# Second layer of a two-layer recurrent and attention network: the pass for row maxima runs nine slots ahead of the scores instead of eight

## The reference

```
xn = layernorm(x)                       # layer 0
s  = selective scan over the 512 tokens, 16 states per feature, gated, projected
g  = silu(mixture of 8 experts, top 2, gelu, 512 wide)
x  = x + s * g
xn = layernorm(x)                       # layer 1
s  = causal softmax attention, one head of 128
h  = xn + latent attention(rmsnorm(xn)) # 16 heads of 64, causal, keys and values from a latent of 16
g  = silu(h + mixture of 8 experts, top 2, 64 wide, and one shared expert, of rmsnorm(h))
x  = x + s * g
```

```
att = q @ k.T / 8 ; att = where(causal, att, -inf)
p   = exp(att - rowmax(att)) ; y = (p @ v) / rowsum(p)
```

## Time and profile before

| | us |
|---|---|
| median of 3 runs | 1270.45 |
| lowest, highest | 1266.95, 1274.91 |
| the profiled execution, its own time | 1278.83 |
| its span, first to last instruction | 1276.9 |
| PE busy in the span | 1093.6 |
| DVE busy | 961.0 |
| ACT busy | 623.0 |
| first scores of slot 0, in the trace | 407.55 |
| exponentials of slot 191, in the trace | 1232.3 |

### The profile page before, as it was taken

One profiled execution on the slowest core, in us unless ns is written; L12 is line 12 of the kernel. 1 busy time (PEld: TensorE's weight loads), 2 busy tenths in 40 slices (PEclk: granted clock), 3 DMA queues, 4 the chain that ended last, 5 costly groups with the idle time before them and its releaser, 6 DMA issues.

```text
span 1276.9 us, 19206 instructions
## 1 busy us (share of the span) xinstructions
PE 1093.6 (86%) x6753; PEld 691.8 (54%) x6753; DVE 961.0 (75%) x1490; ACT 623.0 (49%) x1111; POOL 306.7 (24%) x371
## 2 busy tenths in 40 slices
PE   7669999999676878889788988998998889899897
PEld 6557887888333434544544554464464346446454
DVE  6757887988367886888788798889889878654424
ACT  2647758565323534346545453654553552353531
POOL 2065554551312300410320231032033021000000
PEclk9769999999887789899988988997898999999998
DMA  7667777775325252345325433543433530130010
GB/s 188 188 198 252 227 228 221 233 225 167 117 53 138 77 125 68 94 116 118 101 69 115 126 103 90 113 126 85 99 105 112 110 84 27 37 65 28 16 45 17
DMA packets 97069, 150.24 MB, mean 118 GB/s; under 512 B 26984, under 2 KB 55984, under 8 KB 96912
## 3 DMA queue, kind: packets, MB, share of 16 engines
q1 hardware_dynamic: 73840, 72.33, 22.6%
q0 software_dynamic: 22976, 76.43, 19.6%
q10 hardware_dynamic: 160, 0.26, 0.1%
HBM read 124.33 MB, written 11.54 MB: 106 GB/s over the span
## 4 chain that ended last, share of the span: by engine, by line
PE 37%; DVE 20%; issue 7%; ACT 5%; DMA 2%; POOL 2%; SPq 0%; another core or an unknown queue 0%; DVEq 0%; ACTq 0%; POOLq 0%
PE bank L1245 8%; DVE neg_max L1767 4%; PE bank L1274 3%; PE bank L1325 3%; DVE sc_state L298 2%; PE bank L1339 2%; PE bank L1334 2%; PE bank L1293 2%; ACT probs L1569 2%; PE bank L1251 2%; PE bank L1329 2%; DMA q_all<-turned_rows 2%; PE bank L1253 2%; DVE sc_y L315 1%; PE bank L1316 1%
## 5 line engine op out<-in xcount | busy, mean ns | idle before, releaser
L1569 ACT ACTIVATE probs<-bank 128x1024 f32<-128x1024 f32 (+1 forms) x192 | 169.3, 882 | 285.6 <-PE bank L1251 204.0
L1767 DVE TENSOR_REDUCE neg_max<-bank 128x2 f32<-128x1024 f32 (+3 forms) x256 | 203.4, 815 | 131.4 <-PE bank L1251 81.3
L1245 PE MATMUL bank<-q_all,kk 49*128 49x512 f32 (+3 forms) x1024 | 203.2, 496 | 48.6 <-ACT probs L1569 30.1
L212 POOL DMA_DIRECT2D sc_bc_wide<-scan_bc x128 | 73.0, 572 | 442.8 <-DVE sc_ub L291 238.8
L1245 PEld LDWEIGHTS bank<-q_all,kk 49*128 49x128 f32 x1024 | 86.6, 194 | 150.3 <-ACT probs L1569 56.7
L1293 PE MATMUL bank<-kr,q_all 48*128 48x512 f32 (+3 forms) x512 | 115.5, 487 | 45.5 <-DVE neg_max L1767 45.2
L779 PE MATMUL bank<-xcol,wst 128*128 128x256 f32 x624 | 149.9, 384 | 0.6 <-ACT xcol L841 0.6
L298 DVE TENSOR_TENSOR_SCAN sc_state<-sc_a,sc_ub 128x1024 f32<-128x1024 f32 x64 | 145.9, 2280 | 0.0
L900 POOL DMA_INDIRECT xrow<-sorted_in,token_of x78 | 103.3, 1325 | 121.2 <-PE bank L766 64.1
L779 PEld LDWEIGHTS bank<-xcol,wst 128*128 128x128 f32 x624 | 114.2, 193 | 13.6 <-issue 0.9
L1274 PE MATMUL bank<-probs,vaug 128*32 128x512 f32 (+3 forms) x1024 | 98.9, 484 | 0.0
(11 more groups left out here) (307 smaller groups left out, 1803.5 us busy)
## 6 DMA issues: line engine op xcount, KB each, us to landing
sc_bc_wide<-scan_bc POOLq DMA_DIRECT2D x128, 512.0 KB
wst<-in_wexp SPq DMA_DIRECT2D x39, 512.0 KB
q_all<-q_kind SPq DMA_DIRECT2D x94, 128.0 KB, 4.3
rec_wide<-head_recips SPq DMA_DIRECT2D x31, 256.0 KB
p_t<-gates_turned SPq DMA_DIRECT2D x14, 512.0 KB
sorted_out<-xrow SPq DMA_DIRECT2D x7, 640.0 KB
rows_all<-in_x SPq DMA_DIRECT2D x8, 256.0 KB, 5.6
sorted_in<-rows_all SPq DMA_DIRECT2D x8, 256.0 KB, 5.6
```

What stands on the lines that cost most here:

```text
L1245: mm(bank[1][:, par, at:at + n], kk[rows, b % 2, kt * P:(kt + 1) * P], q_all[rows, quad // 2 % 3, pair, kt * P:L].bitcast(F32), start=(at ...
L1569: af(probs[:, slot % RING, :, 0:width], bank[1][:, :, 0:width], ACT.Exp, scale=0.125).then_inc(s["p_ready"], 1)
L1767: last = v.tensor_reduce(neg_max[:, quad % 2, pr:4:2, i], bank[0][:, :, at:at + (i + 1) * P], AX, ALU.max, negate=True)
```

## The change

LEAD becomes 9. The whole pass for maxima, its reductions, the transposes (L1304), ScalarE's copies (L1581) and the DMAs (L1140) move one slot earlier against everything else; the first maxima come in slot -9, the last in slot 182. The transpose moves from the slots 4 mod 6 to the slots 3 mod 6. In slot 39 of a batch bank 7 is therefore in use by the transpose; the gates 3 and 4 go to banks 5 and 6 in place of 7 and 5, and the first up product to bank 7 in place of 6.

```diff
-LEAD = 8
+LEAD = 9
...
                     if (b := due(slot, "gates_b")) is not None and b < B - 1:
-                        gate_part(b, 3, 7)
-                        gate_part(b, 4, 5)
+                        gate_part(b, 3, 5)
+                        gate_part(b, 4, 6)
                     if (b := due(slot, "ups_a")) is not None and b < B - 1:
-                        up_part(b, 0, 6)
+                        up_part(b, 0, 7)
...
-                        silus(b, 3, 5, (7, 5))
+                        silus(b, 3, 5, (5, 6))
...
-                        hidden(b, 0, 6)
+                        hidden(b, 0, 7)
```

## The result

The changed kernel takes 1287.77 us (median of 4 runs, 1285.61 to 1291.86), beside 1270.1 for the kernel before in the same session (4 runs, 1266.95 to 1274.91). The ratio is 1.0132, with a 95% interval from 1.0098 to 1.0166: slower, where the forecast had 0.7% and no change that could be told. The forecast, 1279, is missed by 8.8 us; the time lies in the range, next to rival 1 (1286.5). In a second session the changed kernel took 1288.88 (1282.34 to 1295.25), ratio 1.0123 [1.0085, 1.016].

What follows compares the result with a forecast made beforehand. The bound was taken as a path crossing between TensorE and VectorE, neither alone. Terms -5.0 - 2.0 + 13.7 + 3.0 - 1.0 + 0.5 = +9.2 us on 1270.45 gave 1279 us, range 1264 to 1290.

Steps and rivals of the forecast that it cites:

- rival 1: Slots 33 to 153, 9 mod 24: the lower clock follows TensorE's idle 2.3 us each time; +16, 1286.5 us, chance 0.22.
- The bank wait: Slots 9 mod 24: `turn2` waits for bank 7 until ScalarE copies the maxima after the exponentials; loss of 13.7 us.
- The clock behind it: Slots 9 mod 24: TensorE's clock may fall after idling, slowing the query products; 0.5 a batch, loss of 3.0 us.
- the gains: Terms outside slots 9 mod 24: DMA waits, clock after slot 24, pairing and start; -7.5 us together.
- DMA waits: Slots 18, 24, 174 and 180: scores wait less for the maxima's rows, sent earlier; gain of 5.0 us.
- clock after slot 24: From 512 to 522 us: without the idle time before it, TensorE's clock stays higher; gain of 2.0 us.
- pairing: VectorE's scan step meets other block widths; a narrow reduction replaces a wide one in slots 28 to 30; gain of 1.0 us.
- start: One more narrow block of maxima ahead of slot 0, one less in slot 183; loss of 0.5 us.
- Slots of 6 mod 24: Waits for the maxima's rows here are covered by VectorE's reduction, so removing them gains 0.
- Rivals 2 and 3: Bank wait covered, 1265.5 us, chance 0.17; that and all DMA waits real, 1254 to 1256 us, chance 0.07.
- Rival 4: New pairing of blocks costs or gives 0.05 us in each of 192 slots, 10 us either way; chance 0.09.
- Rival 5: The rows leave SP hardly earlier in all quads, losing the gain of 5.0 + 2.0; +16 us, chance 0.03.

Runs made afterwards that it cites:

- the filler: The change plus nine unused products of 512 columns into bank 5 in TensorE's idle time ahead of `turn2`, slots 33 to 153; 1280.5 us.
- the last kernel above: The change with transpose, copy and DMAs of quads 2 mod 4 one slot later, and maxima's rows ahead of reciprocals' read on SP; 1270.29 us, ratio 0.9953.
- SP's order: The change with the maxima's rows ahead of the read of the reciprocals in SP's DMA queue; 1289.13 us, ratio 1.0136.

## Why the prediction was too low, and where it was right

**The bank wait: right in place and mechanism.** 13.7 us of idle time predicted, 14.7 measured, by the chain that was worked out from the earlier trace rows. Taking it out gives back the whole loss, and putting it into the kernel before makes the whole loss. By the filler, though, its own worth in time is some 9.

**The clock behind it: too low.** 3.0 predicted (0.5 a batch). In the trace the low clock came in three batches of six and cost 1.57, 1.06 and 1.14 at the query products, 3.8 in all, and 4.7 in the steps. By medians the filler gave back 7.3; the bounds, 0 and 10, held it. The forecast reasoned from the length of the idle time, 2.3 us near 2.52, and the length doesn't decide it: 2.25 us were followed by the full clock in slots 57 and 129 and by the low one in slot 105, and 2.04 us in slot 153 by the low one.

**The two together: right, with luck.** 16.7 predicted, 16.3 measured between the change and the kernel with the quads 2 mod 4 late, split 9 and 7 in place of 13.7 and 3.0: one too high, one too low.

**The step that failed: the gains, -7.5.** They are the sum of DMA waits (-5.0), clock after slot 24 (-2.0), pairing (-1.0) and start (+0.5). Measured as one, without slot 180: -0.2. Had the prediction put 0 there, it would have said 1287.2.
- *DMA waits on the path, and the clock after slot 24.* The numbers came in part: slots 24 to 26 -4.1, slots 174 to 180 -3.2; slot 18 +0.3 in place of -0.6 (-0.5 in the change's second trace). But only slots 174 to 180 came by the reason given. Slots 24 to 26 shorten by 3.7 with the rows as late as before, so the lead did most of it, and that this came to the predicted 4.5 is luck. 1.5 of it, slot 26 at the full clock, also came in the trace of the kernel before with the added wait, where nothing was moved.
- *What ate it:* slot 4 +2.3, slots 28 and 29 +2.7. The text took the maxima's rows for the only DMA in these slots' way, and expected a narrow reduction to help in 28 to 30. VectorE idles there for another DMA, the gathered expert rows, and the reduction in slot 28 is a wide one in place of a narrow one. Where the gathers came in time (the last kernel above), slots 28 and 29 lose 1.2 in place of 2.7, and slots 24 to 26 gain nothing. This is read from the traces; no run moves the gathers, and why they come later in slot 3 stays open.
- *Slots of 6 mod 24*: covered, as the text said, by VectorE and, which it didn't say, by the slot before's exponentials (2.32 us of the 3.46 in slot 78). That the waits would be nearly gone from the table was wrong: SP holds the rows there too, and only its other order takes them away. The rule that the text quoted from the Trainium skill, "DMA: Bandwidth & Descriptors", on issuing early agrees with the trace in this, that rows sent early enough are no longer waited for. The inference that their waits then come off the time does not: 18.6 us of them were worth nothing in one kernel and 15.7 us some 5 in another.

**The chances.** What came is nearest to rival 1, which had 0.22. Its time, 1286.5, fits better than its reason: it had the clock at 10 and kept the gains, where the clock came to some 7, the wait to less than its length, and the gains to nothing. Rivals 2 and 3 fall with the 14.7 us of wait. Rival 4, the shapes, falls with the kernel in which all quads are late. Rival 5 was right in this, that SP held the rows (slot 78), and wrong in what that cost.

## What to carry to other kernels

When a step is moved earlier, count for its new slot the claims on each shared buffer and find who empties them: a second claim waits for the emptier's whole in-order queue, here a copy behind exponentials that wait for a third engine. If there are more claims than banks, another bank may only move the wait (it did here); put the waiting claim behind whatever other engines need (9 us here between the two places) or leave it in its old slot. And a wait's length in a table isn't its worth: before pricing its removal, look up what else the same instruction would have waited for, and which other DMA the shortened slots will run into (here the gathered rows that VectorE needs).

## What the runs showed of the hardware

TensorE's clock after an idle time of 2.0 to 2.6 us is not decided by its length alone. Query products in slots 9 mod 24, six batches each: at the low clock (2.8 to 3.6 us in place of 1.9 to 2.0) in three of six in the change and four of six in its repetition, though the two programs are the same; in four of six with SP's order; in three with the wait put into the kernel before. With 1.69 us of idle time it was one of six, and none of six with SP's order on top; with the filler, or without a wait there, none. Executions of the change lie between 1282 and 1295 us; how much of this spread is the clock was not separated. A term for it needs a range, and one trace isn't a measure of it.
